# A one-column fill on GpSimd, and receiver rows gathered after all sender rows

## What is computed

```python
edge_feat = concatenate([h[dst], h[src], rel_pos, distance], axis=-1)
x = silu(edge_feat @ W1 + b1)
x = silu(x @ W2 + b2)
scores = (x @ W3 + b3)[:, 0]
alpha = softmax of scores over the edges with the same dst
msg = h[src] @ Wv * (alpha * node_weight[src])[:, None]
out = segment_sum(msg, dst)
result = layernorm(h + (h + out), axis=-1)
```

## Time and profile before

| | |
|---|---|
| median of three runs | 1073.45 us |
| the profiled execution, its own time | 1075.52 us |
| its span, first to last instruction | 1073.6 us |
| GpSimd (POOL) busy | 801.6 us, 75% |
| DVE busy | 611.0 us, 57% |
| PE busy | 601.4 us, 56% |
| ACT busy | 516.3 us, 48% |
| mean granted TensorE clock | 0.717 of full |

### The profile page before, as it was taken

The page is one execution under the profiler, slowest core; times in us unless marked ns, Lnnn a source line. Parts: engine busy times, 40 slices in busy tenths (PEclk is TensorE's granted clock), DMA queues, the critical chain, the costliest instruction groups (busy, mean ns, idle before and its releaser), DMA issues.

```text
span 1073.6 us, 11099 instructions
## 1 busy us (share of the span) xinstructions
PE 601.4 (56%) x2391; PEld 349.7 (33%) x2391; DVE 611.0 (57%) x2374; ACT 516.3 (48%) x1217; POOL 801.6 (75%) x877
## 2 busy tenths in 40 slices
PE   1988989997653655666666656676657640000000
PEld 0444445444322323344434434344434340000000
DVE  7888876867327535887888699663424484100000
ACT  0556546554416565778779788854334333000000
POOL 7777777774777777777777777777777777777775
PEclk9988677667556778788878888887877655555555
DMA  6688887886677757678676777632222112111110
GB/s 198 211 312 300 268 286 255 290 303 189 203 226 257 281 197 268 239 267 282 223 271 234 267 249 256 233 116 75 70 71 65 54 41 71 41 41 47 47 46 28
DMA packets 77914, 198.01 MB, mean 184 GB/s; under 512 B 19007, under 2 KB 49409, under 8 KB 65304
## 3 DMA queue, kind: packets, MB, share of 16 engines
q1 hardware_dynamic: 49560, 134.37, 34.7%
q0 software_dynamic: 28288, 62.93, 20.0%
HBM read 106.64 MB, written 92.16 MB: 185 GB/s over the span
## 4 chain that ended last, share of the span: by engine, by line
PE 21%; POOL 21%; DVE 21%; issue 18%; ACT 3%; DMA 2%; POOLq 0%; SPq 0%; DVEq 0%; ACTq 0%
POOL out_rows L419 11%; POOL region L415 5%; PE bank L579 5%; POOL hk L415 4%; DVE dst L890 4%; PE bank L627 4%; PE bank L614 3%; PE bank L621 3%; DVE m_q L964 3%; PE bank L604 2%; ACT xin L475 2%; DVE est L978 2%; DVE hk L973 2%; PE bank L629 1%; DVE xin L905 1%
## 5 line engine op out<-in xcount | busy, mean ns | idle before, releaser
L475 ACT ACTIVATE xin<-xin,drs 128x128 f32<-128x128 f32 x637 | 258.3, 484 | 67.7 <-DVE drs L875 67.7
L419 POOL DMA_INDIRECT out_rows<-hk,sidx_t x196 | 191.0, 974 | 69.1 <-issue 54.1
L415 POOL DMA_INDIRECT hk<-in_x,kg_t x196 | 185.6, 947 | 69.2 <-issue 46.3
L415 POOL DMA_INDIRECT region<-in_xw,snd_t x196 | 189.9, 969 | 62.2 <-issue 49.8
L415 POOL DMA_INDIRECT region<-rec_d,id_t x196 | 186.2, 950 | 62.2 <-issue 58.8
L579 PE MATMUL bank<-wsv,region 128*128 128x256 f32 x392 | 184.5, 564 | 24.1 <-ACT region L484 8.5
L890 DVE BATCH_NORM_STATS2 dst<-xin 128x6 f32<-128x256 f32 x392 | 137.0, 414 | 17.8 <-DMA xin<-in_x 17.5
L964 DVE TENSOR_SCALAR m_q<-bank,kcol,acol 128x128 f32<-128x128 f32 x196 | 75.0, 408 | 115.1 <-PE bank L643 115.1
L604 PE MATMUL bank<-region,m_q 128*128 128x128 f32 x392 | 75.0, 350 | 94.6 <-DVE m_q L964 94.6
L627 PE MATMUL bank<-hkT,w1a 128*128 128x512 f32 x98 | 71.3, 819 | 92.9 <-issue 82.8
L604 PEld LDWEIGHTS bank<-region,m_q 128*128 128x128 f32 x392 | 63.4, 246 | 107.5 <-DVE m_q L964 107.5
(11 more groups left out here) (180 smaller groups left out, 938.2 us busy)
## 6 DMA issues: line engine op xcount, KB each, us to landing
xin<-in_x SPq DMA_DIRECT2D x49, 1024.0 KB, 6.5
out_rows<-xin SPq DMA_DIRECT2D x49, 1024.0 KB, 5.0
rec_d<-region SPq DMA_DIRECT2D x49, 512.0 KB, 6.4
region<-in_xw,snd_t POOLq DMA_INDIRECT x196, 6.0
hk<-in_x,kg_t POOLq DMA_INDIRECT x196, 3.1
region<-rec_d,id_t POOLq DMA_INDIRECT x196, 3.0
out_rows<-hk,sidx_t POOLq DMA_INDIRECT x196, 2.2
ef_d<-hk SPq DMA_DIRECT2D x9, 196.0 KB, 3.4
```

The lines of the kernel that those rows point to most:

```text
L415: pool.indirect_dma_start(out=to, out_offset=None, in_=frm, in_offset=bass.IndirectOffsetOnAxis(ap=index, axis=0)).then_inc(done, 16)
L419: pool.indirect_dma_start(out=out, out_offset=bass.IndirectOffsetOnAxis(ap=index, axis=0), in_=frm, in_offset=None, bounds_check=N - 1, oo ...
L475: ins = nc.scalar.activation(xin[:, j % X_RING, n, :], xin[:, j % X_RING, n, :], ACT.Identity, bias=drs[:, j % 2, 1, n:n + 1], scale=drs[: ...
```

## The change

`HK_FROM` becomes 49, so `pool_plan()` gives hs0 to hs48, hk0 to hk7, and from r0 on the same items in the same places as before. The tile `idle` becomes one column wide; the fills stay where they were in the count of items, 87 of them.

```diff
@@ -71,7 +71,7 @@
 SORT_PLAN, FLIP_TURNS = sort_plan()
 TABLE_TURN = len(SORT_PLAN)
-HK_FROM = TABLE_TURN + 1
+HK_FROM = G
 LEAD = 8
 REST = 20
 B0 = G + 1
@@ -169,7 +169,7 @@
         cwd = sb("cwd", [P, 3, BR])
         cwe = sb("cwe", [P, 3, BT])
-        idle = sb("idle", [P, 512])
+        idle = sb("idle", [P, 1])
```

## The result

The changed kernel took **1037.31 us** in the median of four runs (1031.85 to 1038.89) against 1073.36 us before: 0.965 of it, 95% interval 0.959 to 0.970. The forecast was 1038 us, with a range of 1029 to 1051. One more execution of the changed kernel on record, outside this median, took 1040.24 us.

A forecast was written before the change was run, and what follows sets the result against it. GpSimd's list of 786 transfers was taken to set the time; 9.2 us for the order and 26.0 for the fills make 35.2, so 1040.3 us for the profiled execution and 1038 us for the median, range 1029 to 1051.

The forecast's parts named there:

- What bounds the kernel: Whole kernel: GpSimd's own list of 786 transfers, one after the other at 1.25 or 1.28 us, sets the time.
- The fill's price, 0.44 us: Fills on GpSimd's list: one column saves 0.44 of 0.51 us each; 59 behind r0's start give 26.0 us.
- Rival 1: Fills: the small fill is hardly cheaper, its semaphore wait being the price; 0.1 us saved each, 1059 us; chance 0.07.
- The 22 fills of stage one, worth nothing: Fills before hs44: they save nothing, since 9.7 us would become GpSimd's waits for places of the full ring.
- growing waits for L928 and L492: Stage one, sign in the profile after: GpSimd's waits for L928 and L492 grow by up to 10 us.
- The order, 9.2 us: Ahead of r0: hs45 to hs48 no longer wait behind hk0; r0 at 312.1 us against 321.26.
- the time at which ring places come free: End of stage one: places for hs45 to hs48 come free at 245.1, 253.2, 260.8 and 265.4 us, unchanged.
- The two terms: The forecast's sum: 9.2 us from the order ahead of r0 and 26.0 us from the 59 fills behind it.
- Stage two keeps up: Behind r0: compute follows steps of 10.08 us, 10.5 before; the ring of 12 covers 36 us and could lose 11.
- no wait for L604: Stage two, sign in the profile after: no GpSimd wait for L604 over 1 us.

The follow-up runs named there:

- LEAD = 4: The changed kernel with r0 behind hk3 in place of hk7, 16 gathers earlier; 1048.61 us, 0.978 of before.
- the odd chip: Chip where all kernels were some 20% longer: before 1298.81 us, changed 1275.48 (0.987), changed with 512-column fills up to hs48 1273.38 (0.984).
- the first pair: First profiles of the kernel before and the changed kernel: r0 to the end 752.3 against 728.1 us; profiled executions 1075.52 and 1031.85 us.
- The order alone: The changed kernel with the fill put back to 512 columns, so only the reordering is left; 1065.46 us, 0.992 of before.

## Why the prediction was right

**What bounds the kernel**: right. GpSimd's list of 786 transfers at 1.25 and 1.28 us sets everything from r0 on. Each kernel with the same fills has the same 727 to 728 us there, whatever it does ahead of r0 (LEAD = 4, with four more items behind r0, has 20 us more); the odd chip is the one exception.

**The fill's price, 0.44 us**: measured 24.2 us over 59 fills in the first pair, and 753.0 - 727.5 = 25.5 us by the means of the three profiles with wide fills behind r0 and the seven with small ones, so 0.41 to 0.43 us each. Start to start across a fill behind r0, the medians of the changed kernel's first profile are 1.33 us to gathers and 1.89 to scatters, against 1.76 and 2.31 before. The row's length said 0.543 - 0.118 = 0.425 us; I had taken 0.10 for the small fill, and it is 0.12. The rule of the Trainium skill, page "Perfetto Trace Analysis", section "GPSIMD Engine Instruction", that a row of this sort may not be trusted, asked for care; here row and spacing agree within 0.02 us. Rival 1, that the price is the wait, is wrong for gathers. For scatters it was half right: the 0.5 us of the longer gap come with the fill, as the kernel without fills shows; whether they are the wait for its semaphore was not tested apart. But they are not won by a smaller fill, and the forecast had left them where they are.

**The 22 fills of stage one, worth nothing**: right, within 1 to 3 us that were not resolved. The sign named for it, growing waits for L928 and L492, is blurred, since part of them is put down to "issue" and the row of L492 holds usual gaps. All idle time ahead of sender rows grew from 62.2 us to 68.6, 74.1 and 75.2 in the changed kernel's profiles, hs45 to hs48 among them.

**The order, 9.2 us**: the mechanism is right, the size a little small. The order alone gained 10.3 us by the medians (5.5 to 11.6 by the interval of its ratio). The 9.2 us hold the four small fills between hs48 and r0 as well, worth some 2 us (hs48 to r0 is 47.2 us with the order alone, 45.3 in the changed kernel beside it), so the order alone was forecast at about 7. The term that was off is the time at which ring places come free: forecast hs46, hs47, hs48 and hk0 at 253.7, 261.3, 266.6 and 271.8 us, in the changed kernel's later profiles 250.5 to 251.7, 257.6 to 258.8, 262.6 to 263.9 and 267.6 to 268.9. r0 then lies at 307.9 and 309.2 us in place of 312.1. I had read these places from one execution before, which was 2 us over the median; that may be a part of it. (The forecast's own sum is also 0.4 us long: 261.3 + 5.0 + 0.07 is 266.4, and 5.0 more 271.4.) The two terms miss in opposite ways, 0.5 to 1.8 us too much for the fill and, by this result, 1 to 3 too little for what lies ahead of r0. So it is partly luck that the sum came within 1 us: the changed kernel gained 36.1 us here, and 37.1 and 33.3 in the two later comparisons on other chips, against a forecast of 35.2.

**Stage two keeps up**: right on the chips where the kernel before took some 1073 us; no wait for L604 shows in the profile after. On one chip it did not.

## What to carry to other kernels

Where one engine's list of instructions sets the end, price an edit by start-to-start spacing on that list and count only the places where the engine has nothing to wait for: 87 fills became cheaper here, and the 59 behind r0 counted, with four just ahead of it. Ahead of a ring that is full, a faster producer gained nothing that could be resolved here; what an item waits for there, and what is queued behind it, is worth more than its own length. And judge stretches of a profile apart: 728 us repeated within 1 us in three profiles of the changed kernel, while the 300 us ahead of them moved by 7.

## What the runs showed that I had not expected

- A fill that is waited for costs 0.09 us ahead of a gather and 0.6 us ahead of a scatter, with one column, since the gap behind it is 0.79 us there in place of 0.27. Without the fill the same scatters have 0.30.
- The last record's write took 7.8 us from issue to the release of GpSimd with LEAD = 4, against 3.5 us in the profile before. What made it longer is not shown.
- On one of the four chips of the experiments, all kernels took 1270 to 1300 us, with idle time on ACT and DVE put down to nothing in the kernel, and the same change was worth 1.3% in place of 3.2 to 3.5%.
